# Decay rows repeated over partitions by DMA, and the finish of k and q moved between engines, in a fused linear-attention and expert kernel

## The chip, the cores and the metric

The kernel runs on one core of one Trainium2 chip. The metric is the device time of one launch in microseconds (us), the median of several runs. Engines are named as in the profile: PE is TensorE (PEld its weight loads), DVE is VectorE, ACT is ScalarE, POOL is GpSimd, and SP is the sync engine, which here issues every DMA. S, K, Q, KTR, NUM and DENSE are PSUM banks.

## The reference, cut to what matters

The input x is [8, 2048, 256]. A modulated LayerNorm is followed by linear attention with 16 heads of 64 and a per-head decay, and then by a layer of eight experts of which two are used. Only the attention is touched by the change:

```
q, k = elu(h @ Wq) + 1, elu(h @ Wk) + 1          # h: modulated LayerNorm of x
a    = sigmoid(h @ Wa + ba + 2)                  # one decay per token and head
S_t  = a_t * S_(t-1) + k_t (x) [v_t, 1];  out_t = q_t . S_t, divided by its last column
x   += ga * (out @ Wo)
```

elu(x) + 1 is x + 1 where x is positive and exp(x) elsewhere. The kernel before computes it as relu(x) + exp(-relu(-x)); it is also max(x + 1, exp(-relu(-x))), since exp(x) is at least x + 1 everywhere and x + 1 is at least 1 where x is positive.

## The kernel before

The sequence is cut into 32 groups of 512 tokens (index T), each into four chunks of 128. Heads are taken in pairs, eight pairs (units) to a group, 256 units in all. The attention phase is one program per engine, written out as steps (T, u), u from 0 to 7; each engine runs its part of a step in the order of the code and waits on semaphores. A hardware loop covers two groups a turn. In step (T, u) the engines work on three units at once: unit a, two ahead of the step (projections, decay, scores), unit b, one ahead (output), and unit n of the step itself (transposed output). After the attention, an expert phase runs that the change doesn't touch.

**PE, one step.** K projection (six matmuls of 512 columns into bank K), Q projection into Q, two matmuls that repeat two rows of decays over 128 partitions into the two S banks (L630), a first dense job, one matmul that repeats the running decay products (lam) into Q (L638), the transposes of unit n's output into K (`transpose_o`, L613), the transposes of k into KTR (L648), a second dense job, then the scores of unit a (L670, into the S banks), the part of unit b's output that comes from the states (L680), the part from the scores (L688), and the state updates of unit a (L700)..

**Dense jobs** share the bank DENSE: u=0 two halves of the output projection (wo), u=1 two blocks of v, u=2 two transposes of h, u=3 a v block and z (the decay logits), u=4 a v block and the transposes of the decays (`arow_job`, L544), u=5 and u=6 one v block, u=7 two.

**DVE, one step.** The two decay scans (L839, from the S banks and eye4, into `decay`), the low part of the transposed output (`o_low`, L829), the last columns of lam (L847), the product of lam and q (L852, qs_sb), the scores times decay (L864, p_sb), division of unit b's output (L871, L874, L876), and the chain of four state updates (L817), in every other group with a clamp ahead (L805). In step 0 all LayerNorm statistics of the next group stand in front of this (`ln_stats`), in step 3 `sigmoid_step` is interleaved with the chain, in step 4 `decay_products` (L784) runs as the second dense output.

**ACT, one step.** For K and then for Q: relu(-x), relu(x), exp (`elu_parts`, L427, L428, L430); then the copy of a v block, the high part of the transposed output (L434) and k times decay (L456, kd_sb).

**POOL, one step.** k = k_plus + exp (L360) and q = q_plus + exp (L366); in u=0 also the reciprocal deviation and the residual, in u=1 `ln_apply` (four instructions on 256 columns), in u=2 the low part of h, in u=5 `lam_low` (L345).

A bank is written again only when its readers are done: K by `transpose_o` after `k_pos`, that is after ACT's second pass over K; the next k and decay values likewise.

The two lines of PE that decide the order ahead of the scores read, in the kernel before:

```
pe.wait_ge(k_pos, a + 1)                              # L610, ahead of transpose_o
pe.wait_ge(q_ready, a + 1); pe.wait_ge(decay_ready, 2 * a + 2)     # L655, L656, ahead of the scores
```

Of the kernel before, what the change touches and what calls it, by code (L numbers as in the profile page):

```python
# [52 lines left out]
ROWS = LO + HEADS  # L53
# [72 lines left out]
def adaln_block(nc, x, Wq, Wk, Wv, Wo, Wa, ba, gate_W, gate_b, expert_W, expert_b, c, wmod, out):  # L126
    tokens = x.rearrange("b (g c p) d -> (b g) p c d", p=CH, c=NCH)
    out_tokens = out.rearrange("b (g c p) d -> (b g) p c d", p=CH, c=NCH)
    x1_dram = nc.dram_tensor("x1_dram", [NG, CH, NCH, D], F32, kind="Internal").ap()
    gates_dram = nc.dram_tensor("gates_dram", [2, BATCH, D], F32, kind="Internal").ap()  # L130

    with ExitStack() as keep:
# [5 lines left out]
        attention_phase(nc, tokens, Wq, Wk, Wv, Wo, Wa, ba, c, wmod, x1_dram, gates_dram, mod, ident, bank)  # L138
# [3 lines left out]
def attention_phase(nc, tokens, Wq, Wk, Wv, Wo, Wa, ba, c, wmod, x1_dram, gates_dram, mod, ident, bank):  # L142
    with ExitStack() as ctx:
# [3 lines left out]
        def sem(name):  # L147
            return ctx.enter_context(nc.semaphore(name))
# [11 lines left out]
        head_sel = sb("head_sel", [128, HEADS, DH], F32R)  # L160
        head_sel32 = sb("head_sel32", [128, HEADS])
# [19 lines left out]
        a_cols = sb("a_cols", [128, NCH, ROWS_A + HEADS], F32R)  # L181
        lam_row = sb("lam_row", [HEADS, GT])
        az = [sb(f"az{i}", [128, NCH, CH], F32R) for i in range(2)]
        lam = sb("lam", [128, NCH, CH], F32R)
# [5 lines left out]
        q_plus = sb("q_plus", [128, GT])  # L190
        k_plus = sb("k_plus", [128, GT])
        qs_sb = sb("qs_sb", [128, 2, GT])
        lam_end = sb("lam_end", [128, 2, NCH])
# [28 lines left out]
        z_ps = sem("z_ps"); zb_ready = sem("zb_ready"); z_exp = sem("z_exp"); a_step = sem("a_step"); a_split = sem("a_split"); a_ready = sem("a_ready")  # L222
        arow_ps = sem("arow_ps"); az_ready = sem("az_ready")
        lam_step = sem("lam_step"); lam_hi_ready = sem("lam_hi_ready"); lam_ready = sem("lam_ready")
# [3 lines left out]
        q_ps = sem("q_ps"); q_exp = sem("q_exp"); q_neg = sem("q_neg"); q_pos = sem("q_pos"); q_ready = sem("q_ready")  # L228
        k_ps = sem("k_ps"); k_exp = sem("k_exp"); k_neg = sem("k_neg"); k_pos = sem("k_pos"); k_ready = sem("k_ready")
        abc_ps = sem("abc_ps"); decay_ready = sem("decay_ready")  # L230
        lam_ps = sem("lam_ps"); qs_ready = sem("qs_ready"); lam_end_ready = sem("lam_end_ready")
# [27 lines left out]
        def _(sp):  # L259
# [17 lines left out]
            def step(T, s, u):  # L277
                if u == 0 and exists(T - 1):
                    after(sp, x1_ready, T * 2)
                    sp.dma_start(x1_dram[bass.ds(T - 1, 1)].rearrange("g p c d -> (g p) c d"), x_res[:, :, :])\  # L280
                      .then_inc(x1_stored, 16)
                if u == 0 and exists(T):
# [5 lines left out]
                if u == 4 and exists(T + 2):  # L288
# [4 lines left out]
            attention_steps(sp, step)  # L293
            sp.wait_ge(x1_stored, 16 * NG)

        @block.gpsimd
        def _(pool):
# [4 lines left out]
            def ln_apply(T):  # L302
# [4 lines left out]
                for ch in range(NCH):  # L307
# [6 lines left out]
            pool.memset(head_sel32[:, :], 0.0).then_inc(fills, 1)  # L314
# [5 lines left out]
            pool.wait_ge(fills, 5)  # L320
# [6 lines left out]
            pool.affine_select(out=head_sel32[:, :], in_=head_sel32[:, :], compare_op=ALU.not_equal, fill=1.0,  # L327
                               base=0, pattern=[[-1, HEADS]], channel_multiplier=1).then_inc(fills, 1)
            pool.wait_ge(fills, 6)
            pool.affine_select(out=head_sel32[:, :], in_=head_sel32[:, :], compare_op=ALU.not_equal, fill=1.0,  # L330
                               base=-LO, pattern=[[-1, HEADS]], channel_multiplier=1).then_inc(consts_ready, 1)
# [10 lines left out]
            def lam_low(T):  # L342
                pool.wait_ge(lam_hi_ready, T + 1)
                hi, lo = (lam[at:at + HEADS, :, :].rearrange("r c i -> r (c i)") for at in (0, LO))
                pool.tensor_tensor(lo, lam_row[:, :], hi.bitcast(F32), ALU.subtract).then_inc(lam_ready, 1)  # L345

# [8 lines left out]
            def step(T, s, u):  # L355
                Ta, _, a = unit(T, u, 2)
                if exists(Ta):
# [21 lines left out]
                if u == 5 and exists(T + 1):  # L379
                    if exists(Ta):  # L380
                        pool.wait_ge(q_ready, a + 1)
                    lam_low(T + 1)
                    pool.wait_ge(lam_ready, T + 2)
# [4 lines left out]
        def _(act):  # L388
# [24 lines left out]
            def dense_out(T, s, u, part):  # L413
# [5 lines left out]
                if job == "a":  # L419
                    act.wait_ge(arow_ps, of + 1)  # L420
                    after(act, abc_ps, (of - 1) * PAIRS * 2)
                    act.activation(az[so][0:ROWS, :, :].rearrange("r c i -> r (c i)"), DENSE[0:ROWS, :], ACT.Copy)\
                       .then_inc(az_ready, 1)

            def elu_parts(a, x, t, plus, x_ps, x_neg, x_pos, x_exp):
# [10 lines left out]
            def step(T, s, u):  # L436
                n = T * PAIRS + u
                Ta, _, a = unit(T, u, 2)
                if exists(Ta):

                    after(act, k_ready, a)
# [897 lines left out]
```

## Time and profile before

| | |
|---|---|
| median of 3 runs | 3915.03 us (3913.11 to 3924.04) |
| the profiled execution's own time | 3912.29 us, span of its trace 3910.5 us |
| attention phase | up to about 2980 us of the span |
| PE busy over the span | 3649.8 us (93%) |
| DVE, ACT, POOL busy | 2809.2 (72%), 1801.7 (46%), 1252.5 us (32%) |
| mean granted TensorE clock | 0.986 of 2.4 GHz |
| DMA | mean 26 GB/s |

A timeline row gives the start and the length of an instruction (or of a run of equal ones), and in brackets how long the engine stood idle ahead of it and what it waited for. A length includes the time in the engine's pipe, so two rows that follow each other overlap a little; the distance between two starts is what an instruction costs its queue.

### The profile page before, as it was taken

The numbers are of one execution on the slowest core, as the hardware profiler recorded it, in microseconds if no ns is written. First come the engines' busy times: TensorE is split into PE (matmuls) and PEld (weight loads), VectorE is DVE, ScalarE is ACT, GpSimd is POOL, SyncE is SP. The second block draws the span as 40 slices with busy tenths as digits, with TensorE's granted clock in tenths as the row PEclk, the third lists the DMA queues.
The fourth block names the chain that finished last, engine by engine and source line by source line (L and its number), as shares of the span: only waits on it lengthen the run. The fifth ranks groups of instructions, "written<-read, shape, count | busy, mean of one in ns | idle before, by whom it ended". The sixth has DMA issues, their size and how long they took to land. (4 is left out here: it accounts for less than half of the span.)

```text
span 3910.5 us, 118885 instructions
## 1 busy us (share of the span) xinstructions
PE 3649.8 (93%) x47274; PEld 3099.4 (79%) x47274; DVE 2809.2 (72%) x6741; ACT 1801.7 (46%) x4588; POOL 1252.5 (32%) x1022
## 2 busy tenths in 40 slices
PE   7999999999999999999999999999997999999998
PEld 5888888888878787888887888888886777777777
DVE  5777666666666676767676766666765888888887
ACT  4555555555555555555555555555553111111111
POOL 3333333333333333333333333333331222222222
PEclk9999999999999999999999999999998999999999
DMA  2000000000000000000000000000002011011110
GB/s 93 18 18 18 19 18 19 18 19 19 18 19 18 23 25 19 24 19 18 19 18 19 18 19 18 19 18 19 18 13 72 33 34 44 33 43 38 38 43 22
DMA packets 66322, 101.84 MB, mean 26 GB/s; under 512 B 3737, under 2 KB 56009, under 8 KB 65481
## 3 DMA queue, kind: packets, MB, share of 16 engines
q1 hardware_dynamic: 65736, 93.95, 7.3%
q8 instruction: 379, 6.21, 0.7%
q14 instruction: 207, 1.69, 0.2%
HBM read 60.36 MB, written 33.57 MB: 24 GB/s over the span
## 5 line engine op out<-in xcount | busy, mean ns | idle before, releaser
L360 POOL TENSOR_TENSOR qk_sb<-k_plus,qk_sb 128x512 f32<-128x512 f32 x256 | 330.9, 1293 | 1430.0 <-ACT qk_sb L430 1430.0
L839 DVE TENSOR_TENSOR_SCAN decay<-bank,eye 128x512 f32<-128x512 f32 x512 | 598.3, 1210 | 251.9 <-PE bank L630 251.8
L427 ACT ACTIVATE qk_sb<-bank 128x512 f32<-128x512 f32 x512 | 307.5, 601 | 953.0 <-PE bank L509 953.0
L1177 DVE SCALAR_TENSOR_TENSOR acc<-bank,comb,acc 128x256 f32<-128x256 f32 x1024 | 462.1, 478 | 93.8 <-PE bank L1091 86.9
L456 ACT ACTIVATE kd_sb<-bank,decay 128x64 f32<-128x64 f32 x2048 | 449.9, 333 | 169.3 <-PE bank L648 166.8
L1089 PE MATMUL bank<-ew_hi,h_hi 128*128 128x512 f32 x1024 | 421.1, 411 | 2.1 <-DVE ew_lo L1161 2.1
L1090 PE MATMUL bank<-ew_lo,h_hi 128*128 128x512 f32 x1024 | 408.4, 399 | 0.0
L1091 PE MATMUL bank<-ew_hi,h_lo 128*128 128x512 f32 x1024 | 408.2, 399 | 0.0
L864 DVE TENSOR_TENSOR p_sb<-bank,decay 128x512 f32<-128x512 f32 x512 | 329.4, 685 | 90.2 <-PE bank L670 88.7
L670 PE MATMUL bank<-qk_sb 64*64 64x128 f32 x8192 | 286.8, 275 | 71.3 <-POOL qk_sb L366 57.5
L366 POOL TENSOR_TENSOR qk_sb<-q_plus,qk_sb 128x512 f32<-128x512 f32 x256 | 326.7, 1276 | 47.3 <-ACT qk_sb L430 46.9
L670 PEld LDWEIGHTS bank<-qk_sb 64*64 64x64 f32 x8192 | 227.1, 132 | 132.2 <-issue 132.0
L430 ACT ACTIVATE qk_sb<-qk_sb 128x512 f32<-128x512 f32 x512 | 329.2, 643 | 0.0
L688 PE MATMUL bank_pair<-v_sb,p_sb 128*64 128x65 f32 x8192 | 299.5, 225 | 4.8 <-issue 4.4
L507 PE MATMUL bank<-wo_hi,oT_hi 128*128 128x256 f32 x1024 | 292.2, 285 | 10.3 <-DVE xn L736 8.6
L829 DVE TENSOR_TENSOR oT_lo<-bank,oT_hi 128x512 fp32r<-128x512 f32 x256 | 177.1, 692 | 156.9 <-ACT oT_hi L434 156.9
L509 PE MATMUL bank<-wo_hi,oT_lo 128*128 128x256 f32 x1024 | 289.5, 283 | 0.0
L508 PE MATMUL bank<-wo_lo,oT_hi 128*128 128x256 f32 x1024 | 289.3, 283 | 0.0
L688 PEld LDWEIGHTS bank_pair<-v_sb,p_sb 128*64 128x64 f32 x8192 | 261.8, 137 | 24.5 <-issue 7.0
L507 PE MATMUL bank<-h_hi,wk_hi 128*128 128x512 f32 x512 | 233.2, 456 | 43.1 <-issue 43.1
L736 DVE TENSOR_TENSOR xn<-bank,ga 128x512 f32<-128x512 f32 x64 | 44.3, 692 | 277.5 <-PE bank L509 277.5
L1022 POOL TENSOR_TENSOR acc<-acc,gb 128x512 f32<-128x512 f32 x64 | 82.6, 1291 | 482.9 <-DVE acc L1177 465.7
(193 smaller groups left out, 8619.8 us busy)
## 6 DMA issues: line engine op xcount, KB each, us to landing
x_in<-in_L_attn_x_dram SPq DMA_DIRECT2D x32, 512.0 KB, 3.8
x_res<-in_L_attn_x_dram SPq DMA_DIRECT2D x32, 512.0 KB, 3.8
x_dram<-x_res SPq DMA_DIRECT2D x32, 512.0 KB, 2.7
x<-x_dram SPq DMA_DIRECT2D x32, 512.0 KB, 3.3
out_dram<-x SPq DMA_DIRECT2D x32, 512.0 KB, 2.9
ew_raw<-in_L_ffn_expert_W_dram SPq DMA_DIRECT2D x8, 256.0 KB, 5.0
v_sb<-in_L_attn_Wq_dram SPq DMA_DIRECT2D x1, 1024.0 KB, 8.1
v_sb<-in_L_attn_Wv_dram SPq DMA_DIRECT2D x1, 1024.0 KB, 10.1
```

Source lines behind the costliest of these rows:

```text
L360: pool.tensor_tensor(k_sb, k_plus[:, :], k_sb, ALU.add).then_inc(k_ready, 1)
L430: act.activation(t, t, ACT.Exp, scale=-1.0).then_inc(x_exp, 1)
L456: ins = act.activation(kd_sb[:, ch, hd * DH:(hd + 1) * DH], KTR[:, ch * CH + hd * DH:ch * CH + (hd + 1) * DH], ACT.Copy, scale=decay[:, hd ...
L507: pe.matmul(dst, s_hi, m_hi, start=(n == 0), stop=False)
L670: mm = pe.matmul(S[hd][halves[half], tok], k_sb[rows, keys], q_sb[rows, tok], start=True, stop=True)
L688: mm = pe.matmul(NUM[halves[half], hd, ch * VW:(ch + 1) * VW], p_sb[:, pb % 2, hd, query], v_sb[:, ch, 2 * pb + hd, :], start=False, stop= ...
L839: dve.tensor_tensor_scan(decay[:, hd, :], S[hd][:, :], eye4[:, :, :].rearrange("p c i -> p (c i)"), 0.0, ALU.mult, ALU.add).then_inc(decay ...
L864: dve.tensor_tensor(p_sb[:, na, hd, :], S[hd][:, :], decay[:, hd, :], ALU.mult)\
L1089: pe.matmul(y[:, :], h[:, kt, tok], ew_hi[:, kt, ex, :], start=(kt == 0), stop=False)
L1090: pe.matmul(y[:, :], h[:, kt, tok], ew_lo[:, kt, ex, :], start=False, stop=False)
L1091: mm = pe.matmul(y[:, :], l[:, kt, tok], ew_hi[:, kt, ex, :], start=False, stop=(kt == KT - 1))
L1177: dve.scalar_tensor_tensor(a, y[:, (k // 2) * D:(k // 2 + 1) * D], comb[s % 2][:, 2 * pair + i, e:e + 1], a, ALU.mult, ALU.add).then_inc(y ...
```

## The change

* **Decay rows.** A new DRAM tensor `rows_dram` takes the decays and their running products of a group (two stores by SP in step 5, then a wait for both). For each unit SP loads `a_bc` (two head rows, repeated over 128 partitions, 512 KB) and `lam_bc` (two DMAs of 64 partitions, 128 KB each), double-buffered, one step ahead of the unit's scans. The decay matmuls (L630, L638), the copy of lam's last columns (L847), head_sel, az, lam and the split of the decays into high and low parts go. The scans read `a_bc` in SBUF.
* **k and q.** ACT makes relu(-x) and exp only. DVE makes k and q in one instruction each, straight from the banks K and Q, right behind the two scans. `transpose_o` waits for `k_ready`, now DVE's.
* **qs.** POOL multiplies `lam_bc` and q (both in SBUF).
* **PE order.** The part of unit b's output from the states (L680) comes ahead of unit a's scores (L670).
* **Statistics.** `bn_stats` of the group two ahead, one in each of the steps 4 to 7, the variance in step 7. The loads and stores of x_in, x_res and x1 move to steps 1 and 2.

```diff
 # SP, each step
+                if u == 5 and exists(T + 1):
+                    sp.wait_ge(a_row_ready, T + 2)
+                    sp.dma_start(rows_dram[1 - s, 0], a_row[:, :]).then_inc(rows_stored, 16)
+                    sp.wait_ge(lam_step, (T + 2) * NCH)
+                    sp.dma_start(rows_dram[1 - s, 1], lam_row[:, :]).then_inc(rows_stored, 16)
+                    sp.wait_ge(rows_stored, (T + 2) * 32)
+                if exists(Tc):
+                    if exists(Tb):
+                        sp.wait_ge(state_step, (b + 1) * NCH)
+                        sp.wait_ge(qs_ready, b + 1)
+                    nc_ = pc % 2
+                    heads = slice(2 * pc, 2 * pc + 2)
+                    sp.dma_start(a_bc[nc_][:, :, :], rows_dram[sc, 0, heads, :].partition_broadcast(128)).then_inc(bc_loaded[nc_], 16)
+                    for hd in range(2):
+                        sp.dma_start(lam_bc[nc_][hd * DH:(hd + 1) * DH, :], rows_dram[sc, 1, 2 * pc + hd, :].partition_broadcast(DH))\
+                          .then_inc(bc_loaded[nc_], 16)
-                if u == 0 and exists(T - 1):
+                if u == 1 and exists(T - 1):
...
-                if u == 4 and exists(T + 2):
+                if u == 2 and exists(T + 2):
 # POOL, each step
-                    pool.wait_ge(k_exp, a + 1)
-                    pool.tensor_tensor(k_sb, k_plus[:, :], k_sb, ALU.add).then_inc(k_ready, 1)
...
-                    pool.wait_ge(q_exp, a + 1)
-                    pool.tensor_tensor(q_sb, q_plus[:, :], q_sb, ALU.add).then_inc(q_ready, 1)
+                    pool.wait_ge(bc_loaded[na], (Ta * (PAIRS // 2) + pa // 2 + 1) * 48)
+                    after(pool, num_ps, a - 1)
+                    pool.wait_ge(q_ready, a + 1)
+                    pool.tensor_tensor(qs_sb[:, na, :], lam_bc[na][:, :], q_sb, ALU.mult).then_inc(qs_ready, 1)
 # ACT
                 act.activation(t, x[:, :], ACT.Relu, scale=-1.0).then_inc(x_neg, 1)
-                act.activation(plus[:, :], x[:, :], ACT.Relu).then_inc(x_pos, 1)
                 act.wait_ge(x_neg, a + 1)
                 act.activation(t, t, ACT.Exp, scale=-1.0).then_inc(x_exp, 1)
 # PE
                         if exists(Ta):
-                            pe.wait_ge(k_pos, a + 1)
+                            pe.wait_ge(k_ready, a + 1)
...
                     project(Ta, sa, pa, "wq", Q, q_ps)
-                    pe.wait_ge(az_ready, Ta + 1)
-                    after(pe, p_ready, 2 * a)
-                    for hd in range(2):
-                        hcol = head_sel[:, 2 * pa + hd, 0:1]
-                        pe.matmul(S[hd][:, :], hcol.to_broadcast([128, 128]),
-                                  az[sa][:, :, :].rearrange("r c i -> r (c i)"),
-                                  start=True, stop=True).then_inc(abc_ps, 1)
                 dense_job(T, s, u, 0)
-                    pe.matmul(Q[:, :], head_sel[:, 2 * pa:2 * pa + 2, :].rearrange("r h d -> r (h d)"),
-                              lam[:, :, :].rearrange("r c i -> r (c i)"), start=True, stop=True).then_inc(lam_ps, 1)
 # DVE, each step
-                if u == 0 and exists(T + 1) and not leads(T):
-                    ln_stats(T + 1)
                 if exists(Ta):
                     after(dve, kd_ready, a)
+                    dve.wait_ge(bc_loaded[na], (Ta * (PAIRS // 2) + pa // 2 + 1) * 48)
                     for hd in range(2):
-                        dve.wait_ge(abc_ps, 2 * a + hd + 1)
-                        dve.tensor_tensor_scan(decay[:, hd, :], S[hd][:, :], eye4[:, :, :].rearrange("p c i -> p (c i)"),
+                        dve.tensor_tensor_scan(decay[:, hd, :], a_bc[na][:, hd, :], eye4[:, :, :].rearrange("p c i -> p (c i)"),
                                                0.0, ALU.mult, ALU.add).then_inc(decay_ready, 1)
+                    dve.wait_ge(k_exp, a + 1)
+                    dve.scalar_tensor_tensor(k_sb, K[:, :], 1.0, k_sb, ALU.add, ALU.max).then_inc(k_ready, 1)
+                    dve.wait_ge(q_exp, a + 1)
+                    dve.scalar_tensor_tensor(q_sb, Q[:, :], 1.0, q_sb, ALU.add, ALU.max).then_inc(q_ready, 1)
...
-                    dve.tensor_tensor(qs_sb[:, na, :], Q[:, :], q_sb, ALU.mult).then_inc(qs_ready, 1)
...
+                if u >= NCH and exists(T + 2):
+                    ln_stats(T + 2, u - NCH)
+                    if u == PAIRS - 1:
+                        ln_variance(T + 2)
```

## Rows read from the trace of the kernel before

**Rows 1.** The page: busy time, share and instructions of each engine.

```profile
PE 3649.8 (93%) x47274; PEld 3099.4 (79%) x47274; DVE 2809.2 (72%) x6741; ACT 1801.7 (46%) x4588; POOL 1252.5 (32%) x1022
```

**Rows 2.** Timeline of PE: the decay matmuls of steps 1, 0 and 1.

```profile
1556.89 0.62 PE L630 MATMUL bank<-az,head_sel 128*128 128x512 f32 x2
...
1626.76 0.62 PE L630 MATMUL bank<-az,head_sel 128*128 128x512 f32 x2
...
1646.43 0.62 PE L630 MATMUL bank<-az,head_sel 128*128 128x512 f32 x2
```

**Rows 3.** Timeline of PE, one step with one v block (start, length, idle before).

```profile
1512.21 0.62 PE L630 MATMUL bank<-az,head_sel 128*128 128x512 f32 x2
1512.67 0.39 PE L507 MATMUL bank<-wv_hi,h_hi 128*128 128x512 f32 x1
...
1514.07 0.39 PE L638 MATMUL bank<-lam,head_sel 128*128 128x512 f32 x1
1514.30 0.60 PE L613 MATMUL bank<-ident,o_sb 128*128 128x128 f32 x4
1514.74 0.60 PE L648 MATMUL bank<-ident,qk_sb 128*128 128x128 f32 x4
1515.95 1.10 PE L670 MATMUL bank<-qk_sb 64*64 64x128 f32 x32 [0.62 <-POOL qk_sb L366]
1516.85 0.32 PE L680 MATMUL bank_pair<-carry,qs_sb 64*64 64x65 f32 x8
...
1517.45 1.15 PE L688 MATMUL bank_pair<-v_sb,p_sb 128*64 128x65 f32 x32
```

**Rows 4.** Who waited for whom: total us, times, longest.

```profile
PE bank L670 <- POOL qk_sb L366: 57.5, 96, 1.4
```

**Rows 5.** Timeline of DVE, the end of step 4, without waits.

```profile
1593.37 1.29 DVE L864 TENSOR_TENSOR p_sb<-bank,decay 128x512 f32<-128x512 f32 x2
...
1595.61 0.31 DVE L805 TENSOR_SCALAR carry<-carry,bound,neg_bound 128x65 f32<-128x65 f32 x1
1595.95 0.28 DVE L817 SCALAR_TENSOR_TENSOR s_mid<-carry,lam_end,bank 128x65 f32<-128x65 f32 x1
...
1596.90 0.28 DVE L817 SCALAR_TENSOR_TENSOR carry<-s_mid,lam_end,bank 128x65 f32<-128x65 f32 x1
```

**Rows 6.** Groups of instructions, whole trace: count, busy us, mean ns, idle before.

```profile
L839 DVE TENSOR_TENSOR_SCAN decay<-bank,eye 128x512 f32<-128x512 f32 x512 | 598.3, 1210 | 251.9 <-PE bank L630 251.8
L1177 DVE SCALAR_TENSOR_TENSOR acc<-bank,comb,acc 128x256 f32<-128x256 f32 x1024 | 462.1, 478 | 93.8 <-PE bank L1091 86.9 <-ACT acc L1045 2.9
L743 DVE BATCH_NORM_STATS2 stats<-x_in 128x6 f32<-128x256 f32 x128 | 44.8, 414 | 36.9 <-issue 36.9
L736 DVE TENSOR_TENSOR xn<-bank,ga 128x512 f32<-128x512 f32 x64 | 44.3, 692 | 277.5 <-PE bank L509 277.5
L784 DVE TENSOR_TENSOR_SCAN lam_row<-bank,zero_row 16x128 f32<-16x128 f32 x128 | 44.2, 398 | 1.7 <-PE bank L544 0.7
L1206 DVE TENSOR_TENSOR h_lo<-h,h_hi 128x512 fp32r<-128x512 f32 x64 | 44.0, 688 | 7.0 <-ACT h_hi L1058 4.0
L535 PE MATMUL bank<-wa,h 128*32 128x16 f32 x2048 | 23.9, 186 | 0.8 <-ACT v_sb L400 0.8
L767 DVE RECIPROCAL a_cols<-a_tok 128x64 f32<-128x64 f32 x32 | 17.5, 546 | 0.0
```

**Rows 7.** DMA issues: count, size of one, median us to landing.

```profile
ga<-gates_dram SPq DMA_DIRECT2D x1, 1024.0 KB, 4.7
```

**Rows 8.** Timelines of DVE and POOL, expert phase, around 3328 us.

```profile
3327.74 0.75 DVE L1241 TENSOR_TENSOR first<-first,red 128x32 f32<-128x32 f32 x1
3327.15 1.29 POOL L1022 TENSOR_TENSOR acc<-acc,gb 128x512 f32<-128x512 f32 x1 [15.34 <-DVE acc L1177]
```

**Rows 9.** Timeline of DVE at the start: running products, then the first decay scans.

```profile
40.68 1.38 DVE L784 TENSOR_TENSOR_SCAN lam_row<-bank,zero_row 16x128 f32<-16x128 f32 x4 [0.73 <-PE bank L544]
...
48.41 2.34 DVE L839 TENSOR_TENSOR_SCAN decay<-bank,eye 128x512 f32<-128x512 f32 x2 [3.79 <-PE bank L630]
```

More of the change, by code:

```diff
@@ L180, in attention_phase @@
         a_tok = sb("a_tok", [128, NCH, HEADS])
-        a_cols = sb("a_cols", [128, NCH, ROWS_A + HEADS], F32R)
+        a_cols = sb("a_cols", [128, NCH, ROWS_A + HEADS])
+        a_row = sb("a_row", [HEADS, GT])
         lam_row = sb("lam_row", [HEADS, GT])
-        az = [sb(f"az{i}", [128, NCH, CH], F32R) for i in range(2)]
-        lam = sb("lam", [128, NCH, CH], F32R)
+        a_bc = [sb(f"a_bc{i}", [128, 2, GT]) for i in range(2)]
+        lam_bc = [sb(f"lam_bc{i}", [128, GT]) for i in range(2)]
         oT_hi = sb("oT_hi", [128, PT, GT], F32R)
@@ L293, in _ @@
             attention_steps(sp, step)
+            sp.wait_ge(x1_ready, 2 * NG)
+            sp.dma_start(x1_dram[NG - 1], x_res[:, :, :]).then_inc(x1_stored, 16)
             sp.wait_ge(x1_stored, 16 * NG)
@@ L420, in dense_out, with exp_of_negative @@
                     act.wait_ge(arow_ps, of + 1)
[L421 to L425, printed above, removed]
+                    after(act, rows_stored, of * 32)
+                    act.activation(a_row[:, :], DENSE[0:HEADS, :], ACT.Copy).then_inc(a_row_ready, 1)
+            def exp_of_negative(a, x, t, x_ps, x_neg, x_exp):
                 act.wait_ge(x_ps, a + 1)
                 act.activation(t, x[:, :], ACT.Relu, scale=-1.0).then_inc(x_neg, 1)
-                act.activation(plus[:, :], x[:, :], ACT.Relu).then_inc(x_pos, 1)
                 act.wait_ge(x_neg, a + 1)
@@ L468, in step @@
                     act.activation(a_tok[:, :, :], a_tok[:, :, :], ACT.Exp, scale=-1.0).then_inc(z_exp, 1)
-                if u == 5 and exists(T + 1):
-                    act.wait_ge(lam_step, (T + 2) * NCH)
-                    after(act, lam_ps, (T + 1) * PAIRS)
-                    act.activation(lam[0:HEADS, :, :].rearrange("r c i -> r (c i)"), lam_row[:, :], ACT.Copy)\
-                       .then_inc(lam_hi_ready, 1)
             attention_steps(act, step)
@@ L660, in step @@
                     after(pe, o_ready, b)
-                pe.sem_inc(inputs_seen)
+                    pe.sem_inc(inputs_seen)
+                    for ch in range(NCH):
+                        state = carry[:, sb_, pb, :] if ch == 0 else s_mid[:, pb % 2, ch - 1, :]
+                        for half in range(2):
+                            query = slice(ch * CH + half * HALF, ch * CH + (half + 1) * HALF)
+                            for hd in range(2):
+                                rows = head_rows[hd]
+                                pe.matmul(NUM[halves[half], hd, ch * VW:(ch + 1) * VW], qs_sb[rows, pb % 2, query], state[rows, :],
+                                          start=(ch == 0), stop=False)
                 if exists(Ta):
+                    pe.wait_ge(q_ready, a + 1)
+                    after(pe, p_ready, 2 * a)
+                    pe.sem_inc(inputs_seen)
                     for ch in range(NCH):
@@ L672, in step @@
                 if exists(Tb):
-                    for ch in range(NCH):
-                        state = carry[:, sb_, pb, :] if ch == 0 else s_mid[:, pb % 2, ch - 1, :]
-                        for half in range(2):
-                            query = slice(ch * CH + half * HALF, ch * CH + (half + 1) * HALF)
-                            for hd in range(2):
-                                rows = head_rows[hd]
-                                pe.matmul(NUM[halves[half], hd, ch * VW:(ch + 1) * VW], qs_sb[rows, pb % 2, query], state[rows, :],
-                                          start=(ch == 0), stop=False)
                     pe.wait_ge(p_ready, 2 * b + 2)
@@ L717, in _ @@
                .then_inc(siluT_ready, 1)
[L719 to L722 removed]
+            dve.wait_ge(consts_ready, 7)
+            dve.memset(a_cols[:, :, :], 0.0)
             def split_weight(n):
@@ L882, in step @@
                         sigmoid_step(T + 1, k)
-            ln_stats(0)
+                if u >= NCH and exists(T + 2):
+                    ln_stats(T + 2, u - NCH)
+                    if u == PAIRS - 1:
+                        ln_variance(T + 2)
+            for ch in range(NCH):
+                ln_stats(0, ch)
+            ln_variance(0)
             dve.wait_ge(mod_ps, 1)
```

113 lines of the change are left out of this document (38 added, 75 removed).

## The prediction

> **What bounds the kernel now.** I read the page first. PE is busy 93% of the span, DVE 72%, ACT 46%, POOL 32% [rows 1]: so PE is the engine to follow, and DVE is the one that could take its place. Then the timeline of PE, for the length of a group. The decay matmuls stand once in each step at the same place, so their starts measure steps: from step 1 to the next step 0 seven steps take 69.87 us, and step 0, with its two output projections, takes 19.67 us more; together 89.54 us a group where no loop edge falls in it [rows 2]. Inside a step with one v block PE runs without a gap but for 0.62 us ahead of the scores, where it waits for q from POOL [rows 3]. In the whole trace that wait comes to 57.5 us in 96 cases [rows 4]. So the attention phase is PE's work plus a small wait on the path K, Q, ACT, POOL. Last the timeline of DVE, for what a unit's tail costs it back to back [rows 5], and the groups of instructions, for durations [rows 6].
>
> **What is removed from PE.** Two decay matmuls cost 0.46 us (1512.21 to 1512.67) and the lam matmul 0.23 us (1514.07 to 1514.30), 0.69 us a unit [rows 3]. Over 256 units that is 177 us, and with the 57.5 us of waits for POOL [rows 4] 234 us, if PE stayed the bound all the time. I think that it doesn't.
>
> **What is added to DVE, and where.** Gone are one product of 512 columns (0.69, priced by the product from PSUM, 692 ns) and a short copy; new are two instructions of three operands from PSUM. For these the nearest rows are 478 ns for 256 columns [rows 6] and 0.28 us for 65 [rows 5]: 0.20 us over 191 columns, so 0.75 us for 512 (low 0.69, as a two-operand product; high 0.80). The sum on DVE is only some 0.7 us a unit. The place is what matters. `transpose_o` waited for ACT's second pass over K; now it waits until DVE has made k, and DVE makes k only after the chain of the unit before and two scans. That closes a loop through both engines:
>
> scores landed, then DVE: scores times decay and the division up to the clamp 2.24 (1593.37 to 1595.61), four chain links 1.23 (1595.95 to 1596.90, plus 0.28) [rows 5], two scans 2.3 (1210 ns each, overlapping a little), k 0.75 [rows 6]; then PE: handover 0.05 (an allowance), output transposes 0.44 (1514.30 to 1514.74), k transposes 0.44 (the same form), the part from the states 0.60 (1516.85 to 1517.45), scores 1.10, handover 0.07 [rows 3]. Sum 9.22 us. q (0.75) and the low part of the output lie beside PE's 2.6 us and cost nothing; without that cover they would cost 1.4. ACT's kd lies there too. In the kernel before the first three DVE terms ended before the scans were wanted, and only the scores hung on them.
>
> PE's own work in a step with one v block is about 8.3 us: 69.87 over seven steps [rows 2], less the 4.43 of what single steps have more (the four items below that are PE's, with 1.40 twice), less 7 x 0.69, less 0.62 in the four steps without a second long job, is 58.1, a seventh of it 8.3. So the loop of 9.22 is longer and sets the step. What stands between k and the scores on PE, or on DVE behind the scores, is added to the loop, where before it filled PE: the second v block in steps 1 and 7, 1.40 each (1512.67 to 1514.07) [rows 3]; second h transposes 0.44; z 0.75 (23.9 us over 32 groups) [rows 6]; decay transposes 0.44. On DVE: the sigmoid's reciprocal between the chain links 0.55; running products behind the low part of the output, 1.38 (44.2 over 32), of which I estimate 0.3 to stick out; the spread statistics of steps 4 to 6, 3 x 0.35 (44.8 over 128) [rows 6]. Those of step 7 and the variance fall into step 0, where DVE has much slack. Sum 6.33. The clamp, 0.34 (1595.61 to 1595.95) [rows 5], comes into 3.5 of these seven steps on average: 1.19.
>
> Seven steps: 7 x 9.22 + 6.33 + 1.19 = 72.06 us, against 69.87 before: +2.19. Step 0 is PE's: some 11 us of output projection (19.67 [rows 2] less 8.3) cover DVE. It loses the 0.46 of the decay matmuls; the lam matmul's 0.23 was cover for the wait for `wo_scaled` between the halves and turns into wait. -0.46. Moving the statistics out of step 0 gains nothing, since they were hidden there. A group: +1.73 us; 32 groups: +55 us.
>
> **ACT, POOL, SP.** ACT loses two passes a unit; it wasn't on the path (its two passes over K begin as soon as K is projected, and the chain and the scans take 3.5 us from the step's start on). POOL's qs is wanted only in the next step. SP's loads of a unit are issued when the chain of the unit two before is done, and wanted one loop later, 9.22 us. The nearest row is 1024 KB, also repeated over partitions, landed 4.7 us after issue [rows 7]; here it is 768 KB in three DMAs, which I put at 5 to 6.5 us with their issues (low 4, high 9). Hidden. In step 1, the store of x1 and the load of x_res stand between two such loads on SP, but x_res is issued before the next chain is done.
>
> **Two rules weighed.** In the expert phase a product of 32 columns with both inputs in SBUF took 0.75 us and ended at 3328.49, as POOL's instruction that had begun at 3327.15 ended, at 3328.44 [rows 8]. The Trainium skill, "SBUF — State Buffer", section "Who interferes with whom", says that a DVE instruction with two SBUF inputs and a GpSimd instruction that reads SBUF exclude each other for their whole length. The trace agrees. The scans are of that kind only after the change, since `a_bc` is in SBUF; it is a rival below.
>
> The product from PSUM takes 692 ns, the same with both inputs in SBUF 688 [rows 6]; so I give the scans no gain from SBUF. The Trainium skill, "VectorE: DVE Perf Modes", section on the TRN2 errata, gives a fixed part of 120 cycles from PSUM and 58 from SBUF. By it each scan would be some 0.065 us shorter, an estimate, and the sum 29 us lower. The rows speak against it.
>
> **Start.** The running products end at 42.06 and the first scans begin at 48.41 [rows 9]. Now two stores and their landing (3 us, an estimate below the 4.7 of [rows 7]) and then the loads (5 to 6.5) stand between: about 52. +4 us, between 0 and 8.
>
> Sum: the profiled execution's own 3912.3 + 55 + 4 = 3971 us; the median is 2.7 above that execution, so 3974.
>
> **Price of an error.** 0.1 us on the loop is 7 x 32 x 0.1 = 22 us. k at 0.69 and no handovers: loop 9.04, 3934. k at 0.80 and 0.1 us more at each handover between engines: 9.5, 4036. PE has gaps of its own in some groups (a loop edge, late instructions), which may vanish in the new waits: up to 15 us less. Own range of this case 3925 to 4045.
>
> **Rivals.**
> - *The loop is shorter than I make it, and the sign turns (24%).* Place: the two scans and k between chain and transposes. It decides from 1.73/7 = 0.25 us a unit. For it: no row shows a scan with both inputs in SBUF; 512 columns take 1210 ns where a product takes 692 [rows 6], and if part of that were PSUM's, it would go. At the product's price the loop falls by 1.04: -7.28 + 1.73 = -5.55 a group, 3741 us; at half of that -1.91 a group, 3858. Were DVE never late at all, PE would save 7 x 0.69 + 0.46 + 1.8 (57.5 over 32) = 7.1 a group: 3692. Against it: the running products, 398 ns for 128 columns, and 1210 for 512 [rows 6] give 2.1 ns a column, a rate and not a fixed cost.
> - *It evens out (10%).* The loop is 0.2 to 0.3 us shorter, by handovers and vanished gaps: 3903 to 3927.
> - *The scans are locked out by POOL (10%).* `ln_apply`, four instructions which at the 1.29 us of [rows 8] take 5.2 us, now starts behind qs of step 1, some 7.7 us into it, and ends about where the scans of step 2 begin (10.6 for the step, 2.4 for the chain). If it is later, one to two instructions stand before the scans once a group, 1.3 to 2.6 us: 41 to 83 us more, 4015 to 4057. PE's h transposes then wait as well.
> - *The loads are late (8%).* From 9.2 us after the chain on, each us more costs half a us a unit (two loops go round in the time of a load and a loop): 112 us per us, so 4086 at 10.2. For it: 80 GB/s more traffic, all from the same few rows of DRAM, in front of instruction fetches too. Against: 4.7 us for 1024 KB [rows 7].
>
> **Chances.** Forecast 48%, locked scans 10%, late loads 8%: slower 66%. Within 0.3% (12 us, about what a measurement of this kernel can tell from no change) 10%. Faster 24%: some 14% down to 3850, 10% below it. The range 3850 to 4090 leaves out those 10%, and some 7% above. The likeliest time is 3974.
>
> **What the profile after would show.** Right: PE idle ahead of `transpose_o`, 0.9 to 1.5 us in steps 1 to 7, released by DVE's k; the wait for POOL's q gone; steps with one v block 9.2 to 9.9 us and not shorter than 8.6; step 1 longer than before (10.6 against 10.4); DVE without idle from the scores to k; k and q at 0.75; scans at 1.21; step 0 near 19.2; PE busy under 88% in the attention. Wrong: scans clearly under 1.2 us, or PE idle under 0.5 us ahead of the transposes (then faster); DVE idle ahead of the scans until a DMA (late loads); single scans over 1.3 us in step 2 (lock).

## The result and the profile after

The changed kernel takes 3952.17 us (median of 4 runs, 3945.5 to 3952.74), the kernel before beside it 3916.91 us (3913.11 to 3924.04): ratio 1.0091, 95% interval 1.0076 to 1.0105. It is slower by 0.9%, 35 us. Forecast were 3974 us, a range of 3850 to 4090, and slower at 66%.

The page of the profile after, its head (busy time by engine; DMA traffic, of which the kernel before moved 26 GB/s on average):

```profile
span 3950.6 us, 117499 instructions
PE 3504.8 (89%) x46506; PEld 2916.9 (74%) x46506; DVE 2878.1 (73%) x6705; ACT 1621.8 (41%) x4044; POOL 896.7 (23%) x731
DMA packets 146132, 304.81 MB, mean 77 GB/s; under 512 B 17048, under 2 KB 69320, under 8 KB 145352
```

Against [rows 1], PE has 145 us less work, DVE 69 us more, ACT and POOL 180 and 356 us less, and the span is 40 us longer. No engine's busy share explains that. PE's waits between 80 and 2960 us do (who waited for whom: total us, times, longest):

```profile
PE bank L606 <- DVE qk_sb L811: 229.1, 215, 2.1
PE bank L500 <- issue: 42.3, 13, 3.4
PE bank_pair L663 <- issue: 21.2, 23, 2.4
PE bank L500 <- DVE xn L709: 14.9, 30, 0.5
PE bank L655 <- issue: 12.3, 14, 1.5
```

The wait of [rows 4] is gone. In its place stands one four times as long: the transposes of o (L606) wait for DVE's k (L811) in 215 of 256 steps. A wait for "issue" is one in which PE waited for nothing that the profile shows; the 13 of L500 stand where the hardware loop jumps back, once in two groups (a loop edge), and the kernel before has them too (43.1 us). The groups of instructions (count, busy us, mean ns, idle before):

```profile
L808 DVE TENSOR_TENSOR_SCAN decay<-a_bc,eye 128x512 f32<-128x512 f32 x512 | 595.5, 1205 | 59.3 <-issue 55.4 <-DMA lam_bc<-rows_dram 3.8
...
L813 DVE SCALAR_TENSOR_TENSOR qk_sb<-bank,qk_sb 128x512 f32<-128x512 f32 x256 | 174.2, 681 | 1.6 <-ACT qk_sb L429 1.6
L811 DVE SCALAR_TENSOR_TENSOR qk_sb<-bank,qk_sb 128x512 f32<-128x512 f32 x256 | 170.4, 666 | 0.7 <-ACT qk_sb L429 0.7
```

The scans take 1205 ns from SBUF, where [rows 6] had 1210 from PSUM, and they never wait for a load but once, at the start. One turn of the loop, on DVE and then on PE (start, length, idle before):

```profile
1617.55 0.67 DVE L811 SCALAR_TENSOR_TENSOR qk_sb<-bank,qk_sb 128x512 f32<-128x512 f32 x1
...
1621.03 1.29 DVE L828 TENSOR_TENSOR p_sb<-bank,decay 128x512 f32<-128x512 f32 x2 [0.75 <-PE bank L655]
...
1623.27 0.30 DVE L777 TENSOR_SCALAR carry<-carry,bound,neg_bound 128x65 f32<-128x65 f32 x1
1623.61 0.28 DVE L788 SCALAR_TENSOR_TENSOR s_mid<-carry,lam_bc,bank 128x65 f32<-128x65 f32 x1
...
1624.77 0.42 DVE L715 BATCH_NORM_STATS2 stats<-x_in 128x6 f32<-128x256 f32 x1
1625.10 2.33 DVE L808 TENSOR_TENSOR_SCAN decay<-a_bc,eye 128x512 f32<-128x512 f32 x2
1627.34 0.67 DVE L811 SCALAR_TENSOR_TENSOR qk_sb<-bank,qk_sb 128x512 f32<-128x512 f32 x1
1627.92 0.68 DVE L813 SCALAR_TENSOR_TENSOR qk_sb<-bank,qk_sb 128x512 f32<-128x512 f32 x1
```

```profile
1618.27 0.66 PE L606 MATMUL bank<-ident,o_sb 128*128 128x128 f32 x4 [1.52 <-DVE qk_sb L811]
1618.76 0.60 PE L626 MATMUL bank<-ident,qk_sb 128*128 128x128 f32 x4
1619.29 0.34 PE L643 MATMUL bank_pair<-carry,qs_sb 64*64 64x65 f32 x8
...
1619.81 1.06 PE L655 MATMUL bank<-qk_sb 64*64 64x128 f32 x32
...
1628.07 0.66 PE L606 MATMUL bank<-ident,o_sb 128*128 128x128 f32 x4 [1.26 <-DVE qk_sb L811]
```

Follow it: k at 1617.55, transposes, states part, scores, products at 1621.03, clamp at 1623.27, chain from 1623.61, one statistics instruction, scans at 1625.10, k at 1627.34, transposes at 1628.07. From p_sb to k DVE has no idle at all, and PE stands still for 1.52 and 1.26 us in the two steps shown. The turn took 9.80 us from transposes to transposes, of it 0.34 for the clamp and 0.33 for the statistics: about 9.1 for the bare loop.

### The profile page after: what moved, and what is told of

It reads as the page before. It is cut to its first block and busy times, and to the rows that moved or that the text cites. A ratio compares the mean times of both kernels' runs of the same rounds, so it can differ in the third digit from the quotient of the medians.

```text
span 3950.6 us, 117499 instructions
## 1 busy us (share of the span) xinstructions
PE 3504.8 (89%) x46506; PEld 2916.9 (74%) x46506; DVE 2878.1 (73%) x6705; ACT 1621.8 (41%) x4044; POOL 896.7 (23%) x731
## 5 line engine op out<-in xcount | busy, mean ns | idle before, releaser
L372 POOL TENSOR_TENSOR qs_sb<-lam_bc,qk_sb 128x512 f32<-128x512 f32 x256 | 327.9, 1281 | 1836.9 <-DVE qk_sb L813 1836.9
L808 DVE TENSOR_TENSOR_SCAN decay<-a_bc,eye 128x512 f32<-128x512 f32 x512 | 595.5, 1205 | 59.3 <-issue 55.4
L606 PE MATMUL bank<-ident,o_sb 128*128 128x128 f32 x1024 | 166.5, 285 | 239.1 <-DVE qk_sb L811 236.9
L606 PEld LDWEIGHTS bank<-ident,o_sb 128*128 128x128 f32 x1024 | 108.9, 140 | 330.0 <-DVE qk_sb L811 327.3
L500 PE MATMUL bank<-wo_hi,oT_hi 128*128 128x256 f32 x1024 | 291.8, 285 | 17.6 <-DVE xn L709 16.1
L433 ACT ACTIVATE oT_hi<-bank 128x512 fp32r<-128x512 f32 x256 | 153.0, 598 | 360.6 <-PE bank L606 360.6
L500 PE MATMUL bank<-h_hi,wk_hi 128*128 128x512 f32 x512 | 231.2, 452 | 42.3 <-issue 42.3
```

What stands on the lines that cost most here:

```text
L372: pool.tensor_tensor(qs_sb[:, na, :], lam_bc[na][:, :], q_sb, ALU.mult).then_inc(qs_ready, 1)
L500: pe.matmul(dst, s_hi, m_hi, start=(n == 0), stop=False)
L808: dve.tensor_tensor_scan(decay[:, hd, :], a_bc[na][:, hd, :], eye4[:, :, :].rearrange("p c i -> p (c i)"), 0.0, ALU.mult, ALU.add).then_in ...
```

## The experiments

Each was timed in three rounds beside the kernel before. Ratios are to the kernel before; the changed kernel stands at 1.0091.

**Moving k and q in DVE's order.** Three orders of the same four instructions at the head of DVE's step (scan, scan, k, q in the changed kernel). The first:

```diff
-scan(hd 0); scan(hd 1); k; q
+k; scan(hd 0); q; scan(hd 1)
```

> The changed kernel, with DVE's order at the head of a step turned from scan, scan, k, q to k, scan, q, scan; nothing else differs. Theory (the loop): k is ready about 3.8 us into a step, ahead of PE's arrival at the output transposes (4.3 us), so PE's wait for k goes, the two scans leave the loop, and a step with one v block is set by PE and by ACT's kd behind the second scan, about 9.0 us, one with two v blocks by PE alone, 9.8 to 9.9. Some 5 us a group less than the changed kernel and about 155 to 190 us in all: 3760 to 3800 us. Rival (contention: the repeated loads slow PE's instructions and everything else): the work, the traffic and the waits for instructions are the same, so within 15 us of the changed kernel's 3952.

Measured: 3815.46 us, 0.974 (0.9718 to 0.9762). Faster than the kernel before by 2.6%, and than the changed one by 137 us, from the order alone, with the same loads: the rival, contention, is out. The time is 15 us above the expected range; PE's waits from 80 to 2900 us name where some of it went:

```profile
PE bank_pair L663 <- issue: 36.2, 31, 2.0
PE bank L655 <- issue: 32.1, 14, 2.8
PE bank L675 <- ACT kd_sb L454: 28.1, 52, 0.6
...
PE bank L606 <- DVE qk_sb L808: 11.0, 35, 0.8
```

The wait for k is nearly gone (11.0 us), but the waits inside runs of matmuls have doubled, to 68.3 us, and the state matmuls now wait 28.1 us for `kd_sb`. The second order is `k; scan; scan; q`:

> The changed kernel with VectorE's head in the order k, scan, scan, q; k's place is moved, q stays last. Theory (the loop through both engines binds): the transposes of o and k no longer wait for the two scans (2.3 us); the loop now closes through q: products to clamp 2.24, chain 1.15, k 0.67, scans 2.3, q 0.67, scores 1.06 and handovers 0.1 = 8.2 us against 9.1, so the step falls to what TensorE's own work sets, less than in the order k, scan, q, scan, where q is ready 1.17 us earlier: 3820 to 3870 us. Rival (only q's place matters, k's does not): near 3952. Second rival (k alone is what the order k, scan, q, scan gained by): 3810 to 3822, the same as there.

Measured: 3829.34 us, 0.9775 (0.9747 to 0.9803). As the theory had it, and 123 of the 137 us come from k's place; the 14 us between the two orders are not clear, as their intervals overlap. PE's waits from 80 to 2900 us (the attention ends earlier here) show what replaced the old wait:

```profile
PE bank L655 <- DVE qk_sb L813: 80.2, 128, 1.2
...
PE bank L606 <- DVE qk_sb L808: 6.3, 17, 0.8
```

229.1 us ahead of the transposes became 6.3; the scores now wait for q instead, 80.2 us. The third order is `k; q; scan; scan`:

> The changed kernel with VectorE's head in the order k, q, scan, scan. Theory: both scans end when they did in the order k, scan, q, scan, so kd_sb and the products wait no longer than there; q is ready 1.17 us earlier, but its exponential on ScalarE comes about 1 us after k's, so VectorE idles ahead of q with nothing to do: 3805 to 3840 us. Rival (the wait for the exponential costs VectorE its whole 1 us in each step, 224 us in all, and the loop through kd_sb and the states closes): 3900 or more. Rival (no difference to that order at all, TensorE alone is the bound): 3812 to 3820.

Measured: 4179.32 us, 1.0671 (1.0644 to 1.0699). The theory and the reading of no difference missed. The second reading, a loop through `kd_sb` and the states, had the place right, but put only 1 us a step into it; another cause came on top. One step on DVE:

```profile
1608.36 0.69 DVE L810 SCALAR_TENSOR_TENSOR qk_sb<-bank,qk_sb 128x512 f32<-128x512 f32 x1 [0.76 <-ACT qk_sb L429]
1608.97 3.36 DVE L812 TENSOR_TENSOR_SCAN decay<-a_bc,eye 128x512 f32<-128x512 f32 x2
```

and what stands beside it on the timelines of POOL, ACT and PE:

```profile
1609.13 2.12 POOL L372 TENSOR_TENSOR qs_sb<-lam_bc,qk_sb 128x512 f32<-128x512 f32 x1 [3.26 <-DVE qk_sb L810]
1612.36 1.75 ACT L454 ACTIVATE kd_sb<-bank,decay 128x64 f32<-128x64 f32 x8 [2.88 <-DVE decay L812]
1614.17 0.69 PE L675 MATMUL bank<-v_sb,kd_sb 128*64 128x65 f32 x16 [1.58 <-ACT kd_sb L454]
```

PE's wait for it, from 80 to 2960 us, where the changed kernel had none:

```profile
PE bank L675 <- ACT kd_sb L454: 316.6, 198, 2.4
```

The pair of scans takes 3.36 us and not 2.33: q's end releases POOL's `qs_sb`, which also has two SBUF inputs and takes 2.12 us instead of 1.28. One scan passes, then POOL, then the other scan. The late second scan holds `kd_sb` on ACT, `kd_sb` holds the state matmuls on PE, and behind these stand the next K projection, ACT's exponential and k. That loop took 10.88 us here (L675 at 1603.29 and at 1614.17). In the order k, scan, q, scan POOL's `qs_sb` meets only the second scan, which has begun before it: POOL waits (2115 ns mean), the scans don't (1214).

**A suspected cost put in.** One product of 128 x 256 into an unused tile ahead of the scans:

```diff
+dve.tensor_tensor(extra, eye4[:, 0:2, :], eye4[:, 2:4, :], ALU.mult)
 scan(hd 0); scan(hd 1); k; q
```

> The changed kernel with one more product of 128 x 256 on VectorE ahead of the scans in each of the 256 steps, into a tile that nothing reads: a suspected cost put into the loop. Its duration should be near 0.36 us (half of the 0.69 us of a product of 128 x 512). Theory (loop binds in steps 1 to 7 of all groups): 224 to 256 times its duration, +80 to +95 us, 4030 to 4050 us. Rival (TensorE's own work binds and VectorE has slack, 73% busy): 0 to +20 us, 3952 to 3972.

Measured: 4045.8 us, 1.0316 (1.0291 to 1.034): +94 us on the changed kernel by the medians, +88 by the ratios. The timeline of DVE shows its price:

```profile
1610.01 0.43 DVE L809 TENSOR_TENSOR extra<-eye 128x256 f32<-128x256 f32 x1 [4.26 <-issue]
1610.35 2.33 DVE L811 TENSOR_TENSOR_SCAN decay<-a_bc,eye 128x512 f32<-128x512 f32 x2
```

It puts the scans off by 0.34 us: 76 us over the 224 steps 1 to 7, 87 us over all 256. By the starts of the scores on PE's timeline steps 1 to 7 grew by 88 us in all, and step 0 of the groups without a loop edge, where the prediction has DVE off the path, by nothing (19.02 us both times). So an instruction on an engine that is 73% busy costs at least its full price where it lies in the loop. This is the most direct evidence for the prediction's mechanism.

**Taking the statistics out of the loop.**

```diff
-if u >= NCH and exists(T + 2): ln_stats(T + 2, u - NCH) ...
+if u == 0 and exists(T + 1): for ch in range(NCH): ln_stats(T + 1, ch) ...
```

> The spread of the statistics undone: all four bn_stats and the variance of the next group stand again at the head of step 0 on DVE. Theory: three of the four bn_stats, 0.33 us each, leave the loop of steps 5 to 7, and step 0 has room for all: 1.0 us a group, 32 us in all, 3920 us. Rival (contention, or DVE not on the path): no difference, 3945 to 3960; if statistics in step 0 had cost the kernel before something, slower, 3960 to 4000.

Measured: 3931.38 us, 1.0042 (1.0028 to 1.0057): 21 us less. The prediction had priced the statistics at 3 x 0.35 x 32 = 34 us; 0.33 apart in the timeline, they come to 32. By the starts of the scores steps 5, 6 and 7 are 0.32, 0.32 and 0.30 us shorter, as the theory has it. Against that stand 13 us more in step 0, all in groups with a loop edge; but the variants that leave the statistics where the changed kernel has them (order k, scan, q, scan; scores first; the added product) show 8 to 12 us more there too, so this isn't the statistics' price.

**Taking PE work out of the loop.** The scores ahead of the states part, as in the kernel before:

```diff
-NUM = qs_sb x state (L643); S = k_sb x q_sb (L655)
+S = k_sb x q_sb; NUM = qs_sb x state
```

> The changed kernel with TensorE's scores ahead of the part with the states, as in the kernel before; VectorE unchanged. Theory (loop): the states part (0.52 to 0.60 us) leaves the loop between k and the products, 9.11 becomes 8.55, of which up to 0.5 us a step shows: 224 x 0.2 to 0.5 = 45 to 110 us, 3840 to 3907 us. Rival (the order is free, as an average over a bound engine has it): 3947 to 3957. Rival on the other side (the numerator comes later, o with it, and the transposes wait longer): 3965 or more.

Measured: 3894.42 us, 0.9935 (0.9913 to 0.9957): 58 us less than the changed kernel and 0.65% less than the kernel before. One reordering of PE's queue, no work removed, turns the sign of the whole change. It gave half of what 0.52 us in 224 steps would be (116 us), and not in every step: by the starts of the scores steps 2 and 3 are 0.61 and 0.80 us shorter, steps 5 and 6 as long as they were (9.83 and 9.74 against 9.87 and 9.69). Of the 58 us, 14 are shorter waits for "issue" behind the transposes (19.7 against 33.5 us), which the loop doesn't explain.

**The decays by DMA alone**, k and q finished on ACT and POOL as in the kernel before:

```diff
-dve: k = max(K + 1, exp), q = max(Q + 1, exp);  pool: qs = lam_bc * q
+act: plus = relu(x);  pool: k += k_plus, q += q_plus;  dve: qs = lam_bc * q
```

> One part alone: the decay rows by DMA, the PE order and the spread statistics of the changed kernel, but k and q finished as in the kernel before (three passes on ACT, two sums on POOL, output transposes behind ACT's second pass over K), qs on DVE from lam_bc. Theory (the loop through DVE's k): with k off DVE the loop is gone; PE keeps the 0.69 us a unit that the matmuls gave, except where the scores wait for POOL's q, which comes at 6.6 us: steps with one v block near 9.1 instead of 9.7, with two near 9.75. About 4 to 5 us a group below the kernel before: 3750 to 3800 us. Rival (contention by the loads): as slow as the changed kernel, 3930 to 3970.

Measured: 3939.72 us, 1.0056 (1.0037 to 1.0076). The theory missed by 140 us and more; why, the timelines of DVE and POOL show:

```profile
1610.01 3.35 DVE L811 TENSOR_TENSOR_SCAN decay<-a_bc,eye 128x512 f32<-128x512 f32 x2
1610.04 2.23 POOL L368 TENSOR_TENSOR qk_sb<-k_plus,qk_sb 128x512 f32<-128x512 f32 x1 [6.28 <-ACT qk_sb L431]
1612.24 2.18 POOL L373 TENSOR_TENSOR qk_sb<-q_plus,qk_sb 128x512 f32<-128x512 f32 x1
```

The scans, once fed from SBUF, and POOL's sums lock each other out: 3.35 us for two scans, 2.2 us for a sum of 1.29; over the whole trace 1566 ns a scan, and 1711 and 1757 ns a sum. That agrees with the Trainium skill, "SBUF — State Buffer", section "Who interferes with whom", by which the two exclude each other for a whole instruction. PE then waits for k and q from POOL, 108.6 and 74.6 us.

**k and q on DVE alone**, in the kernel before (decays by PE, statistics in step 0, scores first):

```diff
-act: plus = relu(x);  pool: k += k_plus, q += q_plus
+dve, behind the scans: k = max(K + 1, exp), q = max(Q + 1, exp)
```

> The kernel before (decay rows by TensorE, statistics in step 0, scores first) with one part of the change: k and q finished on VectorE behind the two scans, ScalarE's second relu and GpSimd's two sums dropped. Theory: here TensorE's product for lam, ahead of the transposes, writes q's bank and so waits for q (0.67 us behind k), and VectorE's own work up to the products (oT_lo, lam_end, qs_sb) comes behind the transposes: the loop grows by about 0.7 + 0.4 us over the 9.1 of the changed kernel, to about 10.1 us: 224 x 0.5 to 0.9 above the kernel before = 110 to 200 us, 4025 to 4120 us, so this part pays only with the decays loaded by DMA. Rival (it is the part that gains, by taking away GpSimd's 1.29 us at each of k and q, and the DMA part loses): below 3900. Rival (it costs what the change cost): 3940 to 3965.

Measured: 4611.45 us, 1.1756 (1.1727 to 1.1786). The sign was right, the size four times too small. One step on DVE, q to q, and on PE:

```profile
1799.39 0.68 DVE L834 SCALAR_TENSOR_TENSOR qk_sb<-bank,qk_sb 128x512 f32<-128x512 f32 x1
...
1810.82 2.34 DVE L829 TENSOR_TENSOR_SCAN decay<-bank,eye 128x512 f32<-128x512 f32 x2 [1.42 <-PE bank L620]
1813.07 0.67 DVE L832 SCALAR_TENSOR_TENSOR qk_sb<-bank,qk_sb 128x512 f32<-128x512 f32 x1
1813.66 0.68 DVE L834 SCALAR_TENSOR_TENSOR qk_sb<-bank,qk_sb 128x512 f32<-128x512 f32 x1
```

```profile
1800.22 0.47 PE L628 MATMUL bank<-lam,head_sel 128*128 128x512 f32 x1 [2.07 <-DVE qk_sb L834]
...
1810.39 0.62 PE L620 MATMUL bank<-az,head_sel 128*128 128x512 f32 x2
```

I had left out that the scans' input comes from PE here, behind the projections of K and Q. So the loop holds PE's work from the lam product (1800.22) to the decay matmuls (1811.01), then the scans, k and q, with almost nothing beside one another: 14.27 us for this step, part of it at the lower clock (the whole trace has 0.923, the kernel before 0.986). In the changed kernel the scans start at the end of the chain and run beside the projections. So k and q on DVE need the decays from DRAM: without them they cost 17.6%, and on top of them 0.35%.

**How much the traffic itself costs.** The same DMAs, with 4 and 2 rows of each tile loaded in place of 128 and 64, so the decays of the other rows are stale and the output is not the reference's:

```diff
-a_bc[...] <- rows.partition_broadcast(128);  lam_bc[...] <- row.partition_broadcast(64)
+a_bc[0:4] <- rows.partition_broadcast(4);    lam_bc[2 rows] <- row.partition_broadcast(2)
```

> The changed kernel with the same three DMAs a unit, but only over 4 and twice 2 partitions from the third unit on: the other partitions keep the decays of the first two units, so the output isn't the reference's, and 1.5% of the load traffic is left. Waits and issues are the same. Theory (the loop): the loads are hidden, only the longer waits of PE for its instructions (0.7 to 2.3 us, once in most groups) may shrink: 3930 to 3950 us. Rival (contention is what costs): the whole loss and more comes back, 3900 us or less.

Measured: 3935.05 us, 1.0055 (1.0038 to 1.0072), 17 us less, with 28 GB/s in place of 77. PE's waits in the same window:

```profile
PE bank L607 <- DVE qk_sb L812: 233.0, 217, 2.1
...
PE bank L656 <- issue: 8.2, 9, 1.2
PE bank_pair L664 <- issue: 2.8, 10, 0.6
```

The wait for k is what it was. What shrank is the time in which PE, inside a run of matmuls, waited for nothing that the profile shows: 11.0 us against 33.5. Instruction fetches that stand behind the loads would look so, but the profile doesn't name them, and the traffic alone doesn't set these waits: with all the loads, over all matmuls from the transposes to the state updates, they were 73.5 us in the order k, scan, q, scan, 19.7 with the scores first and 18.3 in the order k, q, scan, scan; without any of the loads, in the kernel before, they were 22.2. The cause of the 17 us is open. The reverse, the kernel before with the loads added and unused, wasn't tried.

**Which parts add up.** The order k, scan, q, scan with the statistics in step 0, and then with the scores first as well (diffs as above):

> The changed kernel with VectorE's head in the order k, scan, q, scan (3815) and the statistics back in step 0. Theory: the loop no longer binds in most steps, so the 0.34 us that steps 4 to 7 lose count less than the 21 us that they gave in the changed kernel: 3795 to 3812 us. Rival (the gains add): 3790 to 3797. Rival (step 0 pays for the statistics and nothing is given back): 3815 to 3825.

Measured: 3803.52 us, 0.9714 (0.9691 to 0.9737): as expected, but the 12 us to the order alone are not clear, as the two intervals overlap.

> As the kernel with the order k, scan, q, scan and the statistics in step 0, and TensorE's scores ahead of the part with the states. Theory: q is ready before the transposes end, so the scores don't wait, but the states part is out of the loop; with the loop hardly binding it gives a fraction of the 58 us that it gave in the changed kernel: 0 to 20 us less than without it, 3780 to 3810 us. Rival (the gains add): 3735 to 3750. Rival on the other side (the numerator comes later, and no loop is left to gain from): 3820 or more.

Measured: 3763.89 us, 0.9595 (0.9573 to 0.9616), the fastest of all: 4.0% below the kernel before and, by the two ratios, 4.9% below the changed one. The scores' place gave 40 us more, where I expected 0 to 20. PE's waits for k and q (to 2900 us; L642 are the scores here) are down to this:

```profile
PE bank L642 <- DVE qk_sb L815: 28.1, 66, 0.7
...
PE bank L606 <- DVE qk_sb L811: 11.0, 35, 0.8
```

The same two parts on the order k, scan, scan, q:

> The changed kernel with the order k, scan, scan, q (3829), the statistics in step 0 and the scores ahead of the states part. Theory: here the scores wait for q (80 us in 128 steps with the states part as their cover); without that cover they wait about 0.5 us longer, which eats what the products gain: 3815 to 3850 us. Rival (the gains add): 3750 to 3765. It has no meeting of GpSimd's qs_sb with the scans: if that meeting is what limits the order k, scan, q, scan, this one is the faster of the two.

Measured: 3902.89 us, 0.9969 (0.9957 to 0.998), 74 us slower than that order without them, and 50 us above my range. Here the states part was the cover under which q was made:

```profile
PE bank L642 <- DVE qk_sb L816: 174.3, 155, 1.5
```

174.3 us of waiting for q against 80.2. The scores' place gives 58 and 40 us where q is ready before the scores are due; where both scans stand between k and q, it takes 74, together with the statistics in step 0.

## Why the prediction was right

The mechanism was the predicted one, and four runs hold it up: a cost put in the loop came out at its full price or a little above (+88 to 94 for 76 to 87), two costs taken out of it (statistics, states part) gave 21 and 58 us, and taking the scans from between chain and k gave 137. The size came out near by some luck, as errors of both signs met. Step lengths below are distances between the starts of the scores on PE's timeline, averaged over all groups. Point by point:

- **PE loses 0.69 us a unit.** 177 us by the forecast, 145 us less busy on the page. Of the 32 us between, 25 are in the matmuls that now stand behind the wait: output transposes 166.5 us busy for 153.3, k transposes 157.1 for 153.6, the first states product of a unit 90.1 for 81.7. The lower clock adds little: 0.984 of the span for 0.986.
- **PE's own work, 8.3 us.** The prediction took off 0.62 us in four steps, 2.5 a group, where the 57.5 us of [rows 4] are 1.8 a group. So it is 8.4, still shorter than the loop, and the forecast doesn't change.
- **The loop, 9.22 us.** Measured 9.1. k is 0.67 long, not 0.75 (q follows 0.58 after its start); the states part 0.52 and not 0.60; the chain 1.16 and not 1.23; the scans 2.24 and not 2.3; against that the two sets of transposes take 1.02 and not 0.88, and the handover from the scores to DVE is 0.16. At 22 us per tenth, as the prediction has it, this is some 25 us less.
- **Seven steps, +2.19.** They took +2.2. The same number, but composed otherwise, and that is luck: by the measured loop +1.4 was due, and some +0.8 a group, 25 us in all, come from elsewhere. 11 us are longer waits for "issue" behind the transposes (33.5 us against 22.2), which the prediction didn't have; the rest is open.
- **Step 0, -0.46.** Measured -0.63 in the groups without a loop edge and -1.5 in the others, so about 19 us more gain than forecast. Some 12 of them belong to this kernel's loop edges alone: with the order k, scan, q, scan, with small loads, with the scores first and with the added product, step 0 takes 8 to 15 us more in all, none of it in the groups without an edge. The runs don't tell why.
- **Start, +4.** The first scans wait 3.79 us for lam_bc and begin at 48.90, against 48.41 [rows 9]; the first scores, 52.71 against 51.37, are 1.3 us later. The forecast was +4, so 3 us too much; the stores and loads were quicker than allowed for:

```profile
48.90 2.34 DVE L808 TENSOR_TENSOR_SCAN decay<-a_bc,eye 128x512 f32<-128x512 f32 x2 [3.79 <-DMA lam_bc<-rows_dram]
```

- **The sum.** Forecast +59. Take off 25 for the loop, 19 for step 0 and 3 for the start, add 25 for what was not foreseen: +37. At the last scores the changed kernel's trace is 37.4 us behind, and the medians are 35 apart. So the forecast was 22 us high: 47 us too much for loop, step 0 and start, of which 25 were hidden by an error the other way.
- **Rivals.** The shorter loop through cheaper scans: no, 1205 ns. Evening out: no. Late loads: no; they land 3.4 and 3.8 us after issue, where 5 to 6.5 were allowed and 9.2 were there:

```profile
a_bc<-rows_dram SPq DMA_DIRECT2D x256, 512.0 KB, 3.4
lam_bc<-rows_dram SPq DMA_DIRECT2D x512, 128.0 KB, 3.8
```

Locked scans: not in the changed kernel (1205 ns mean; `ln_apply` took 1227 ns an instruction, 1225 before), and POOL's `qs_sb`, released by q, meets PSUM-fed work. But the lock is real: the scans of two variants ran into it, through POOL's sums and `qs_sb`, not through `ln_apply`, which the prediction had in mind.
- **What the profile was to show.** Idle of 0.9 to 1.5 us ahead of the transposes: 229.1/215 = 1.07 on average, at most 2.1. DVE without idle from the scores to k: yes. The wait for POOL's q gone: yes. k and q at 0.75: no, 0.67 and 0.68. Steps with one v block 9.2 to 9.9 us: yes, steps 5 and 6 are 9.87 and 9.69. PE under 88% in the attention: 2487 us of the stretch from 100 to 2900, 89%; it was 2658, 95%. So 88% was missed by a point. Step 0, where no loop edge falls in it, 19.02 us (forecast near 19.2), step 1 in the same groups 10.51 against 10.42 before: yes.

What stays open: what the longer waits for "issue" are, what the rest of the 0.8 us a group is, and step 0.

## What to carry to other kernels

Before moving work to an engine with slack, write down the loop that it joins: every instruction between one use and the next on all engines, from the timeline. What lies in it can cost its whole length, whatever the busy shares say, and reordering can then give more than moving work did: here the same instructions gave from 3764 to 4179 us. And an order that is right for one loop is wrong for the next one, so reorder and measure together (scores first: -58, -40 and, with the statistics moved as well, +74 us).

## What the runs showed of the hardware

- **The clock after a short wait.** PE had idled 1.98 us ahead of the transposes and then ran at the lower of its two levels, 1.2 GHz. The timeline, and the windows of a stretch ahead and of this one (the seventh item is the granted clock):

```profile
1584.75 0.66 PE L606 MATMUL bank<-ident,o_sb 128*128 128x128 f32 x4 [1.98 <-DVE qk_sb L811]
1585.24 1.01 PE L626 MATMUL bank<-ident,qk_sb 128*128 128x128 f32 x4
```

```profile
1580.00:1582.00 2.00, 2.00 (x10) 1.59 (x10) 1.86 (x7) 1.00 (x2) 0.54 (x1) 1.00 0.29 101
1585.00:1588.70 3.70, 3.70 (x60) 3.37 (x62) 0.98 (x2) 2.96 (x11) 2.51 (x2) 0.54 0.58 186
```

A granted clock of 1.00 and then 0.54, nearly all of it at 1.2 GHz, and four k transposes in 1.01 us instead of 0.60. A wait inside the loop so can cost twice. In the changed kernel that is rare, for PE waited for k 215 times and the clock of the whole trace is still 0.984, against 0.986 before. Where PE waited longer it was lower: 0.959 in the order k, q, scan, scan (316.6 us for `kd_sb`) and 0.923 with k and q alone on DVE (478.9 us for q).
- **Who waits at the lock.** The engine that has begun goes through, and the record of the other grows: 2115 ns for `qs_sb` in the order k, scan, q, scan, where it comes second to a scan, 1281 in the changed kernel, where it meets none.
- **Repeated rows are cheap to load.** 512 KB spread over 128 partitions from two rows of DRAM landed in 3.4 us after issue (median of 256), less than the two 512 KB loads of x in the same kernel did (4.7 and 3.8).
